# A two-layer graph network on one core: the reload of rows between the layers is started under another condition and split otherwise over two queues, one store moves ahead of an exponential, and TensorE's waits for the reload are spread

## The reference

```python
z = h
for l in range(2):
    weights = softmax(z @ envW[l] + envb[l])              # 4 experts
    agg = scatter_mean(z[col], row, N)                    # mean of the neighbours' rows
    combined = concatenate([agg, z], axis=-1)             # 512 features
    outputs = einsum('nd,kdo->nko', combined, W[l]) + z[:, None, :]
    z = relu(einsum('nk,nko->no', weights, outputs))
return x + z
```

## Time and profile before

| | |
|---|---|
| median of 3 runs | 1840.04 us |
| span of the profiled execution, first to last instruction | 1839.2 us |
| granted TensorE clock, mean | 0.969 |
| TensorE matmul busy | 1598.5 us, 87% |
| VectorE, ScalarE, GpSimd busy | 895.0, 572.7, 1214.2 us |
| DMA moved | 393.34 MB, mean 214 GB/s |

### The profile page before, as it was taken

The page is one execution under the profiler, slowest core; times in us unless marked ns, Lnnn a source line. Parts: engine busy times, 40 slices in busy tenths (PEclk is TensorE's granted clock), DMA queues, the critical chain, the costliest instruction groups (busy, mean ns, idle before and its releaser), DMA issues. The chain is left out here.

```text
span 1839.2 us, 36146 instructions
## 1 busy us (share of the span) xinstructions
PE 1598.5 (87%) x8502; PEld 1124.8 (61%) x8503; DVE 895.0 (49%) x2024; ACT 572.7 (31%) x1254; POOL 1214.2 (66%) x1187
## 2 busy tenths in 40 slices
PE   1059999999999999999998389999999999999998
PEld 1036665666666666666665266666666666667665
DVE  6665565655565565555564224334443333443333
ACT  4414333334434333433333022222222222222222
POOL 1377776766776676676663677666666666666764
PEclk9989999999999999999999599999999999999999
DMA  7877766666666666666656987677777777777775
GB/s 218 284 216 227 215 206 186 189 180 195 206 191 197 193 175 194 205 195 197 193 173 215 382 259 244 214 221 220 220 221 222 220 220 220 219 216 215 225 219 150
DMA packets 160202, 393.34 MB, mean 214 GB/s; under 512 B 36989, under 2 KB 61080, under 8 KB 160180
## 3 DMA queue, kind: packets, MB, share of 16 engines
q0 software_dynamic: 92544, 302.70, 55.2%
q10 hardware_dynamic: 35112, 61.46, 9.4%
q1 hardware_dynamic: 32524, 28.91, 5.1%
HBM read 347.61 MB, written 45.37 MB: 214 GB/s over the span
## 5 line engine op out<-in xcount | busy, mean ns | idle before, releaser
L713 POOL DMA_INDIRECT ring<-zp_dram,gather_idx x1152 | 1196.1, 1038 | 535.8 <-issue 271.6
L1333 PE MATMUL agg_ps<-zp,stage 128*128 128x258 f32 x1568 | 447.3, 322 | 23.6 <-PEq L101 23.6
L1366 PE MATMUL mix_ps<-w_sb,turned_m 128*128 128x512 f32 x784 | 405.4, 617 | 16.0 <-PEq L101 14.8
L1295 PE MATMUL agg_ps<-ring,onehot 128*128 x1248 | 398.5, 346 | 23.8 <-PEq L101 17.0
L1366 PE MATMUL mix_ps<-w_sb,turned_z 128*128 128x512 f32 x784 | 400.9, 611 | 10.8 <-PEq L101 10.8
L1335 PE MATMUL agg_ps<-zp,stage 128*128 128x256 f32 x1568 | 384.6, 281 | 0.0
L1075 ACT ACTIVATE stage<-counts_sb 128x512 fp32r<-128x512 uint8 (+1 forms) x416 | 247.1, 605 | 387.5 <-ACTq L101 386.6
L1333 PEld LDWEIGHTS agg_ps<-zp,stage 128*128 128x128 f32 x1568 | 296.1, 189 | 87.7 <-issue 83.9
L1300 PE MATMUL agg_ps<-ring,onehot 128*128 x1248 | 328.2, 289 | 0.0
L1335 PEld LDWEIGHTS agg_ps<-zp,stage 128*128 128x128 f32 x1568 | 296.4, 189 | 34.5 <-issue 34.5
L1295 PEld LDWEIGHTS agg_ps<-ring,onehot 128*128 128x128 f32 x1248 | 242.7, 194 | 79.2 <-issue 73.1
(11 more groups left out here) (157 smaller groups left out, 944.4 us busy)
## 6 DMA issues: line engine op xcount, KB each, us to landing
ring<-zp_dram,gather_idx POOLq DMA_INDIRECT x1152, 3.8
zp_dram<-zp SPq DMA_DIRECT2D x7, 1792.0 KB, 7.3
a_dram<-counts_sb ACTq DMA_DIRECT2D x16, 784.0 KB, 4.9
zp_dram<-parts ACTq DMA_DIRECT2D x49, 256.0 KB
zp<-zp_dram SPq DMA_DIRECT2D x4, 1792.0 KB, 16.3
counts_sb<-a_dram ACTq DMA_DIRECT2D x17, 400.0 KB, 6.4
parts<-in_x ACTq DMA_DIRECT2D x48, 128.0 KB
counts_sb<-a_dram ACTq DMA_DIRECT2D x16, 384.0 KB, 5.4
```

What stands on the lines that cost most here:

```text
L713: pool.indirect_dma_start(out=ring[:, k, t, 0:2 * D].bitcast(F32), out_offset=None, in_=zp_dram[l], in_offset=bass.IndirectOffsetOnAxis(ap ...
L1295: mm = pe.matmul(agg_ps[:, bank, 0:D + 2], onehot[:, place, t, :], rows[:, :, D:2 * D + 2], start=place == 0 and t == 0, stop=True, skip_g ...
L1333: pe.matmul(agg_ps[:, bank, 0:D + 2], stage[:, g % 2, i, :], zp[:, c, D:2 * D + 2], start=c == 0, stop=True, skip_group_check=True)
L1366: mm = pe.matmul(mix_ps[i][:, :], (turned_z, turned_m)[what][:, c, :], w[:, i * HALF:(i + 1) * HALF], start=what == 0 and c == 0, stop=wha ...
```

## The change

Four edits:

1. ScalarE adds one to `s_zkept` ahead of layer 1, so that each take of it by SP needs one round less.
2. `FIRST_GROUPS` goes from 4 to 3: SP reloads groups 0 to 2, and ScalarE's queue groups 3 to 6. VectorE waits for 0 to 2 in slot 0 and for 3 to 6 in slot 1.
3. After the loop of layer 1 the store of the last dense block comes ahead of `exps` and `scale_z`.
4. TensorE waits for a reload group in the `group_sum` that first reads it, no longer for all seven ahead of `product(0)`.

```diff
-FIRST_GROUPS = 4
+FIRST_GROUPS = 3
...
                     act.sem_inc(s_hls, 16)
+                    act.sem_inc(s_zkept, 1)
...
                         copy_mean()
+                        if first:
+                            finish(l, act.snap(dense_no(act, act.snap(rounds - 1)) + SPARSE))
                         exps()
                         scale_z(l)
-                        if first:
-                            finish(l, act.snap(dense_no(act, act.snap(rounds - 1)) + SPARSE))
                         begin(l)
                         finish(l, blk)
...
+                    def rows_of_group(g):
+                        return (min((g + 1) * STAGE, NB) - 1) // LOAD
+
                     def group_sum(l, g, bank):
                         take(pe, s_staged)
+                        if l and (g == 0 or rows_of_group(g) > rows_of_group(g - 1)):
+                            pe.wait_ge(s_zload[rows_of_group(g)], 16)
...
                         logits_of(l)
-                        if l:
-                            for g in range(XG):
-                                pe.wait_ge(s_zload[g], 16)
                         product(0)
```

## The result

The changed kernel took 1844.56 us, the median of 11 runs (1843.31 to 1846.43), beside 1840.55 us for 11 runs of the kernel before on the same chip (1838.01 to 1842.00). The ratio that comes with the runs is 1.0024, with an interval of 1.0015 to 1.0033 (the two medians alone give 1.0022). The medians differ by 4.0 us. Its profiled execution has a span of 1842.0 us, 2.8 more than before, and that same execution lasted 1844.12 us. The mean granted clock was 0.968.

A forecast was written before the change was run, and what follows sets the result against it. TensorE, busy 87% of the span, was taken as the bound, so edits pay only where it stands still. +2.2 - 0.8 + 1.5 = +2.9 us gave span 1842.1, plus 0.8 is 1842.9, say 1843.0; range 1837.0 to 1846.2.

The forecast's parts named there:

- The store at 1000.8: End of layer 1: ScalarE's moved store of the last dense block leaves at about 1000.8 instead of 1003.22, 2.4 us earlier.
- g: Between the layers: how much earlier T0 comes, forecast 3.0 us, bounds 0 and 4.7.
- The counts at 1076.4: ScalarE's queue: the second half of layer 2's first counts lands at 1076.4, counted by bytes, instead of 1070.05.
- T0: Between the layers: when ScalarE issues the weights and the gathers start, 1019.3 before, forecast 1016.3.
- +2.2 for the group sum: First dense slot of layer 2: TensorE's first group sum starts at 1077.1, 2.2 us later than 1074.90.
- -0.8 for the third group: First dense slot of layer 2: TensorE's 0.80 us wait ahead of the third group disappears.
- +1.5 for the clock: After TensorE's idle time ahead of the first group sum: some 3.1 us of work at half clock lose 1.55 us.
- ScalarE's longer issuing: Slot 0 of layer 2: `copy_mean` some 6 us later, covered by the gathers' pace; 0, up to 2 us uncovered.
- counts in time: Rival: ScalarE's queue catches up, counts land no later than before, TensorE keeps all of g; 1837.0 us, chance 0.12.
- half of it: Rival: ScalarE's queue makes up 3.2 us, not 6.4; counts land at 1073.2, group sum 1.0 us earlier; 1839.0, chance 0.20.
- The store lands no sooner: Rival: T0 stays at 1019.3, DMA engines idle 4.3 us, counts land at 1079.5; 1846.0 us, chance 0.15.
- the stores land very soon: Rival: T0 at 1010.2, g 9.1 us, gathers delay ScalarE's queue, counts land at 1080.8; 1847.3 us, chance 0.05.

The follow-up runs named there:

- e7: Kernel before, SP taking `s_zkept` and `s_zused` once instead of in 16 passes, adds only in the last round behind a branch: 1839.00 against 1840.90 us.
- e1: Kernel before with only the last dense store moved ahead of the exponentials: 1840.51 against 1839.93 us, ratio 1.0003.
- e2: Kernel before with only `FIRST_GROUPS` = 3, the fourth reload on ScalarE's queue: 1847.64 against 1839.93 us, ratio 1.0040.
- e5: Changed kernel with `FIRST_GROUPS` back at 4, four reloads on SP: 1839.94 against 1840.78 us for the kernel before, ratio 0.9996.
- e11: Changed kernel with x and first counts ahead of ScalarE's reloads (branch per round), four reloads on SP, no spare add: 1841.72 us, ratio 1.0006 to the kernel before.
- e12: Changed kernel with the first block's x and counts ahead of ScalarE's reloads, a branch in each round: 1842.25 against 1840.78 us for the kernel before.
- e6: Changed kernel with both halves of the first counts ahead of ScalarE's reloads, a branch in each round: 1843.54 against 1840.78 us for the kernel before.
- e16: Kernel before with single waits and ScalarE's three reloads issued by SP behind its first gathers, store in its old place: 1849.98 us, ratio 1.0052.
- e14: Kernel before with early store, single waits and ScalarE's three reloads issued by SP behind its first gathers: 1849.89 against 1840.90 us, ratio 1.0047.
- e15: Kernel before with an always-taken branch around ScalarE's loads in slot 0 of each layer 2 round: 1844.12 against 1840.90 us, ratio 1.0020.

## Why the prediction was right

The forecast was 1843.0 with a range of 1837.0 to 1846.2, and its likeliest case is the one that came: 1844.56. Step by step:

- **The spare add: 0.** It held in the changed kernel and alone (1.0002). SP was late for the 16 passes that it has to count, which e7 confirms: without them its reload left 5.7 us earlier (992.37 against 998.06), though layer 1 ended 1.0 later.
- **The store at 1000.8.** Aligned it left at 1000.84. It landed in 6.2 us where I took 7.1, the second in 6.7 as taken, so g was 3.9 instead of 3.0. I had held SP's fourth issue for a part of the first store's 7.7 us; e1, with 6.4 us beside that issue, and e2, with 7.7 us without it, show that it is none. In all traces that store takes 6.2 to 6.4 us where it leaves early and 7.4 to 8.1 where it leaves late (e7, where the reloads left earlier, apart); why stays open.
- **The counts at 1076.4.** Measured 1076.6, aligned. The way by bytes held: 0.41 MB missing around T0 where I took 0.50, and 3.9 x 209.5 GB/s = 0.82 MB for the gathers where I took 0.63. 1.23 MB at 176.5 GB/s are 7.0 us, 1077.0, 0.4 too much. That the gathers took just 209.5 GB/s has a reason which I had not given: in 1034:1054 GpSimd starts one every 1.25 us, 16 of them moving 4.19 MB, and it does so in the changed kernel too (4.17 MB in the same window). So the gathers went at GpSimd's pace there, and ScalarE's queue got what was left. The gathers' part is what e1 shows alone (no reload moved, the counts some 4 us later), and the reload's part is e2 (no store moved, the passage 4.7 longer).
- **+2.2 for the group sum.** Measured +2.7. TensorE stood for 5.8 us (forecast 4.7); 0.9 of the difference is g.
- **-0.8 for the third group.** The wait went, but this was worth more: before, the third group began 1.82 us after the start of `product(2)`, now 0.46, which is -1.4. The profile counts idle time from the end of a matmul, while a successor that doesn't wait begins before that end.
- **+1.5 for the clock.** From the first group sum to the start of `product(2)` it took 1082.09 - 1076.67 = 5.4 us; before it took 1078.31 - 1074.90 = 3.4. That is +2.0. The clock was at its lower level until about 1081.8, for 5.1 us of work and not 3.1. The two errors nearly cancel, and that is luck: from the first group sum to `product(3)` it took 8.19 us against 7.49, +0.7, as in the sum.
- **ScalarE's longer issuing: 0.** `copy_mean` came 6.4 us later (aligned 7.3):

```profile
1058.24 0.38 ACT L1117 ACTIVATE turned_m<-turn_ps 128x256 f32<-128x256 f32 x1 [41.13 <-ACTq L101]
```

TensorE's last product of slot 0 nevertheless started at 1069.74, aligned 1070.7, against 1074.36: it kept 3.7 of the 3.9 us of g. The cover held.
- **The single waits: 0.** This held alone (1.0008, an interval that begins at 0.9999) and in e5. The last reload landed at 1070.9 and the counts at 1075.7, 4.8 us apart where I had 4.7, so the counts did hide it. (The wait stood ahead of `product(0)`, at 1074.36, so the last reload had been in time by 9.1 us and not by 9.6.) The rounds grew by 0.3 us in the changed kernel, inside the bound of 1.9.
- **From span to time.** The traces differ by 3.7 us aligned, where the sum said 2.9, and the medians by 4.0. I set the runs 0.8 us above the span. As said at e2, the whole time lies about 2 us above it, so by an estimate the profiled execution of the kernel before lasted about 1841.2, some 0.7 above its median of 1840.55. That would account for most of the 0.9 us by which its layer 1 ended later. The forecast is not hurt by it, since it comes to the median before plus the sum.

I gave "within 0.2%" more chance than "slower", and at 1.0024 it is slower. The bound lies in the middle of the forecast case's own range; its place in it was not to be told from these rows.

Of the rivals, "counts in time" is refuted by the wait of 5.8 us, and "half of it" by the counts at 1076.6 and a group sum that came later and not earlier. "The store lands no sooner" is refuted by T0, and "the stores land very soon" by 6.2 and 6.7 us. What decides was named: T0 is worth nothing while the counts decide. e11 and e12 show that it is worth 3.6 us once they don't. By the rule of the Trainium skill in "DMA: Bandwidth & Descriptors", section "Issuing engines are not separate DMA queues", the move of a reload to another engine would have cost nothing. Its first half agrees with these runs (386 and 387 GB/s); e2 shows what this reading leaves out, the order within a queue.

Open stays why layer 1 ended 1.0 to 2.5 us later in the kernels that have a branch only in layer 2 (the 2.5 are of e6, whose profiled execution lay 2.9 above its median); without a branch that moment spreads over 1.4 us, from 993.16 to 994.60.

## What to carry to other kernels

When the DMA engines are full, a transfer that is moved to another queue changes nobody's bytes but everybody's order: ask which transfer its new queue delivers behind it, and how much slack that one has. An event that is brought forward pays only if what ends last comes with it; here the earlier gathers alone used up the slack of the counts. Before an order is mended with a branch in a loop, price the branch: 16 times 0.2 us was nearly the whole gain. And before two traces are subtracted, look where each profiled execution lies among the runs of its kernel.

## What the hardware showed that was not expected

- A store of 0.26 MB takes 6.2 to 8.1 us (the first one) or 5.6 to 6.8 (the second) from issue to the end of the wait for it in the kernels with SP's loop of 16 passes; with empty DMA engines the second one takes 3.3 us (e7).
- An issue isn't over when it is given: four reloads of 1.8 MB held ScalarE for 25.7 us and the counts behind them for 12.6. On SP the fourth one is what turns 3.4 us into 10.3, and a small load of lists behind further reloads held it for 10.5 us (e16) and 13.7 (e14). A store from another engine passes beside such an issue (e1).
- In e14 three queues with work got equal numbers of packets (306, 305, 311), so a transfer in packets of 1 KB fell behind ones of 2 and 3.3 KB: the weights took up to 34.1 us there, 10.5 in the changed kernel and 13.0 before.
- A taken branch with its comparison on ScalarE cost the kernel 0.2 us in each round (e15), though ScalarE is busy for only 31% of the span.
- The granted clock fell from 1.00 to 0.50 at about 1075, some 4 us into the 5.8 us without work, and was back at about 1081.8, after 5.1 us of work. Before the change it was back after some 3 us of work, at about 1072.2.
